# Message layers of a four-part graph network: fewer numbers read per group, SyncE waiting for the messages, and two matrix products per group that nobody reads

## The reference

```python
# layer 0
messages = relu(concat([x[source], x[target]]) @ W_msg + b_msg)
agg_sum = segment_sum(messages, target); counts = segment_sum(1, target)
# layer 1
messages = x[source] * norm[:, None]          # norm = deg_inv_sqrt of both ends
aggregated = segment_sum(messages, target)
```

## Time and profile before

| | us |
|---|---|
| median of 3 runs | 4893.81 (4892.45 to 4899.64) |
| the profiled execution | 4893.52 |
| its span, first to last instruction | 4891.7 |
| edge stage of layer 0, PE's first to last product | 672.9 to about 1222 |
| edge stage of layer 1, PE's first to last product | 1606.3 to about 1921 |

### The profile page before, as it was taken

The page is one execution under the profiler, slowest core; times in us unless marked ns, Lnnn a source line. Parts: engine busy times, 40 slices in busy tenths (PEclk is TensorE's granted clock), DMA queues, the critical chain, the costliest instruction groups (busy, mean ns, idle before and its releaser), DMA issues. The chain is left out here.

```text
span 4891.7 us, 53308 instructions
## 1 busy us (share of the span) xinstructions
PE 3136.8 (64%) x11864; PEld 1962.7 (40%) x11864; DVE 2778.7 (57%) x6341; ACT 968.3 (20%) x1858; POOL 2766.3 (57%) x2438
## 2 busy tenths in 40 slices
PE   4665745556796898766777577777636665655424
PEld 1223534445675787542222244555412222222213
DVE  7996742222455543666777458778755655444323
ACT  0332410000222220221222133333311221111100
POOL 0672057776111771327777588777327776787631
PEclk8876655555555555555555555555568887676665
DMA  6323621111554111551222423433212121333215
GB/s 257 74 70 126 251 83 24 24 24 20 144 151 134 26 26 41 196 188 38 41 41 42 62 44 85 100 78 77 75 47 37 36 37 33 31 30 29 24 15 108
DMA packets 337010, 363.26 MB, mean 74 GB/s; under 512 B 236961, under 2 KB 268843, under 8 KB 336864
## 3 DMA queue, kind: packets, MB, share of 16 engines
q1 hardware_dynamic: 219890, 261.92, 16.6%
q0 software_dynamic: 94096, 80.75, 13.5%
q10 hardware_dynamic: 22878, 18.95, 1.2%
HBM read 188.08 MB, written 188.36 MB: 77 GB/s over the span
## 5 line engine op out<-in xcount | busy, mean ns | idle before, releaser
L784 PE MATMUL e_ps<-e_msg,e_hot 128*128 x2408 | 571.2, 424 | 218.4 <-issue 212.6
L784 PEld LDWEIGHTS e_ps<-e_msg,e_hot 128*128 128x128 f32 x2408 | 530.1, 329 | 297.0 <-issue 297.0
L1674 POOL DMA_INDIRECT u_a<-attended,dst_end x392 | 487.2, 1243 | 146.7 <-issue 116.8
L2310 PE MATMUL d_pl<-d_hot,d_fields 128*65 128x512 f32 x712 | 481.5, 840 | 0.0
L757 DVE TENSOR_TENSOR sums<-e_ps,sums 128x455 f32 (+1 forms) x172 | 108.1, 629 | 552.8 <-PE e_ps L784 552.8
L700 POOL DMA_INDIRECT e_msg<-from_src,e_src x200 | 192.1, 961 | 290.2 <-DMA e_first<-lot_first 231.2
L2254 POOL DMA_INDIRECT flows<-d_out,d_end x160 | 263.9, 1649 | 106.4 <-issue 101.4
L1965 POOL DMA_INDIRECT list<-s_rec,s_place x200 | 199.4, 997 | 215.4 <-DVE s_place L1881 158.5
L2241 POOL DMA_INDIRECT d_near<-term,d_rec x196 | 191.5, 977 | 156.1 <-DMA d_rec<-list 96.7
L879 POOL DMA_INDIRECT a_ends<-h,a_src x200 | 216.2, 1081 | 103.2 <-issue 55.2
L1366 ACT ACTIVATE u_zt<-u_pt 128x256 f32<-128x256 f32 (+1 forms) x392 | 162.7, 431 | 560.8 <-PE u_pt L1266 560.6
(11 more groups left out here) (368 smaller groups left out, 7519.3 us busy)
## 6 DMA issues: line engine op xcount, KB each, us to landing
u_z<-h SPq DMA_DIRECT2D x28, 896.0 KB, 6.3
x<-sums SPq DMA_DIRECT2D x28, 896.0 KB, 7.9
u_x<-x SPq DMA_DIRECT2D x28, 896.0 KB, 7.5
terms<-s_zeros SPq DMA_DIRECT2D x16, 812.5 KB
s_key_row<-src_key SPq DMA_DIRECT2D x50, 256.0 KB
h1d<-u_h SPq DMA_DIRECT2D x14, 910.0 KB, 9.5
u_z<-h1d SPq DMA_DIRECT2D x14, 910.0 KB, 4.6
term<-u_h SPq DMA_DIRECT2D x14, 910.0 KB, 3.7
```

What stands on the lines that cost most here:

```text
L784: last = nc.tensor.matmul(to, hot[s][:, q, :], rows, start=False, stop=q == LOT - 1)
L1674: pool.indirect_dma_start(A[s][:, j, :], None, net.attended[:, :], bass.IndirectOffsetOnAxis(ap=net.dst_end[:, tile:tile + 1], axis=0)).th ...
L2310: last = nc.tensor.matmul(pl[0:WEIGHT + 1, :], fields[:, j, :], hot[:, j, :], start=j == 0, stop=j == J - 1)
```

## The change

The change has four parts, all in the edge stage and in the table that it reads.

1. The plan holds for each item the block number times 65 (`CV1`, the width of a row of `e_msg`), and PE reads only these seven numbers per group. The slot of item q is q minus the difference of its block number to that of the first item, so it is worked out in the register operations that every product has ahead of it anyway. For this the slots in PSUM are 65 columns wide in layer 1 too, and the clearing product writes 455 columns there, where it wrote 448.
2. The chunk number is read by SP, which waits for `msg_ready` and then counts the group in a new semaphore, `lot_ready`; PE waits for that.
3. In layer 1, PE issues 16 products ahead of the first group and two behind every group, each of bf16 ones and zeros (`identb`) with 512 columns, into a PSUM bank of their own (`unread`) that nobody reads.
4. DVE reads the 65-wide slots of a bank with their last column left out in layer 1.

```diff
+CV1 = C + 1
+def fill(nc, net, bank, count):
+
+    for _ in range(count):
+        nc.tensor.matmul(bank[:, :].rearrange("p (r c) -> p r c", c=P), net.identb[:, :],
+                         net.identb[:, :].unsqueeze(1).to_broadcast([P, J, P]), start=True, stop=True)
...
-                nc.vector.tensor_copy(lots[:, :, 0:LOT], block_in)
-                nc.vector.tensor_tensor(lots[:, :, LOT:2 * LOT], tile_in, tile_in[:, :, 0:1].to_broadcast([1, LOTS, LOT]), ALU.subtract)
+                nc.vector.tensor_scalar(lots[:, :, 0:LOT], block_in, float(CV1), None, ALU.mult)
+                nc.vector.tensor_copy(lots[:, :, LOT:2 * LOT], block_in)
...
-def lot_items(nc, pe, plan, g):
-
-    row = plan[0:1, g * PLAN:g * PLAN + 2 * LOT]
-    _, at = nc.values_load_multi_w_load_instructions(row, engines=(nc.tensor.engine,), min_val=0, max_val=BLOCKS - 1,
...
-    chunks = pe.value_load(plan[0:1, g * PLAN + CHUNK_AT:g * PLAN + CHUNK_AT + 1], min_val=1, max_val=CHUNKS)
-    return at[0:LOT], [u.with_bounds(min_val=0, max_val=LOT - 1) for u in at[LOT:2 * LOT]], chunks
+def lot_items(nc, plan, g):
+
+    row = plan[0:1, g * PLAN:g * PLAN + LOT]
+    _, rows = nc.values_load_multi_w_load_instructions(row, engines=(nc.tensor.engine,), min_val=0, max_val=CV1 * (BLOCKS - 1),
...
+    slots = [0] + [(CV1 * q + rows[0] - r).with_bounds(min_val=0, max_val=CV1 * (LOT - 1)) for q, r in enumerate(rows)][1:]
+    return rows, slots
...
+                sp.wait_ge(loaded, 16 * n_loads)
+                for g in range(LOTS):
+                    chunks = sp.value_load(plan[0:1, g * PLAN + CHUNK_AT:g * PLAN + CHUNK_AT + 1], min_val=1, max_val=CHUNKS)
+                    sp.wait_ge(msg_ready, chunks)
+                    sp.sem_inc(lot_ready, 1)
...
-                    nc.vector.tensor_tensor(here, ps[s][:, 0:LOT * wide].rearrange("p (u c) -> p u c", c=wide), here, ALU.add)
+                    nc.vector.tensor_tensor(here, ps[s][:, 0:LOT * CV1].rearrange("p (u c) -> p u c", c=CV1)[:, :, 0:wide], here, ALU.add)
...
-                blocks, slots, chunks = lot_items(nc, pe, plan, 0)
+                blocks, slots = lot_items(nc, plan, 0)
                 for g in range(LOTS):
...
-                    nc.tensor.matmul(ps[s][:, 0:LOT * wide], net.ones3[:, :], nothing[:, 0:LOT * wide], start=True, stop=False)
+                    nc.tensor.matmul(ps[s][:, 0:LOT * CV1], net.ones3[:, :], nothing[:, :], start=True, stop=False)
                     pe.wait_ge(hot_ready, g + 1)
-                    pe.wait_ge(msg_ready, chunks)
+                    pe.wait_ge(lot_ready, g + 1)
                     pe.sem_inc(pe_turn, 1)
...
+                    if g == 0 and not two:
+                        fill(nc, net, unread, 16)
...
                     last.then_inc(multiplied, 1)
+                    if not two:
+                        fill(nc, net, unread, 2)
```

More of the change, by code:

```diff
@@ L343, in _ @@
                     nc.vector.scalar_tensor_tensor(lane_of[:, part], tile_of[:, part], float(-P), spread_dst[:, n, 0:wide], ALU.mult, ALU.add)
-                block_in, tile_in = (row[0:1, 0:LOTS * LOT].rearrange("o (g q) -> o g q", q=LOT) for row in (block_of, tile_of))
-                nc.vector.tensor_copy(lots[:, :, 0:LOT], block_in)
-                nc.vector.tensor_tensor(lots[:, :, LOT:2 * LOT], tile_in, tile_in[:, :, 0:1].to_broadcast([1, LOTS, LOT]), ALU.subtract)
+                block_in = block_of[0:1, 0:LOTS * LOT].rearrange("o (g q) -> o g q", q=LOT)
+                nc.vector.tensor_scalar(lots[:, :, 0:LOT], block_in, float(CV1), None, ALU.mult)
+                nc.vector.tensor_copy(lots[:, :, LOT:2 * LOT], block_in)
                 nc.vector.tensor_copy(first_of[:, :], tile_of[0:1, 0:ITEMS:LOT])
                 v.drain()
-                nc.vector.tensor_scalar(lots[:, :, CHUNK_AT + 1], lots[:, :, LOT - 1], 2, None, ALU.logical_shift_right)
+                nc.vector.tensor_scalar(lots[:, :, CHUNK_AT + 1], lots[:, :, 2 * LOT - 1], 2, None, ALU.logical_shift_right)
                 v.drain()
@@ L672, in edge_sums @@
         ps = [ctx.enter_context(nc.psum_tensor(f"{n}ps{s}", [P, 512], F32)) for s in range(2)]
+        unread = ctx.enter_context(nc.psum_tensor(f"{n}unread", [P, 512], F32))
         if two:
@@ L774, in _ @@
                     pe.wait_ge(placed, g + 1)
-                    nc.tensor.matmul(ps[s][:, 0:LOT * wide], net.ones3[:, :], nothing[:, 0:LOT * wide], start=True, stop=False)
+                    nc.tensor.matmul(ps[s][:, 0:LOT * CV1], net.ones3[:, :], nothing[:, :], start=True, stop=False)
                     pe.wait_ge(hot_ready, g + 1)
-                    pe.wait_ge(msg_ready, chunks)
+                    pe.wait_ge(lot_ready, g + 1)
                     pe.sem_inc(pe_turn, 1)
-                    by_slot = ps[s][:, 0:LOT * wide].rearrange("p (u c) -> p u c", c=wide)
+                    if g == 0 and not two:
+                        fill(nc, net, unread, 16)
                     now = zip(blocks, slots)
+                    all_rows = msg[:, :, :].rearrange("p b c -> p (b c)")
                     for q, (b, u) in enumerate(now):
-                        rows = msg[:, bass.ds(b, 1), 0:wide].rearrange("p b c -> p (b c)")
-                        to = by_slot[:, bass.ds(u, 1), :].rearrange("p u c -> p (u c)")
+                        rows = all_rows[:, bass.ds(b, wide)]
+                        to = ps[s][:, bass.ds(u, wide)]
                         last = nc.tensor.matmul(to, hot[s][:, q, :], rows, start=False, stop=q == LOT - 1)
                         if q == LOT - 2 and g + 1 < LOTS:
-                            blocks, slots, chunks = lot_items(nc, pe, plan, g + 1)
+                            blocks, slots = lot_items(nc, plan, g + 1)
                     last.then_inc(multiplied, 1)
+                    if not two:
+                        fill(nc, net, unread, 2)
 def attention_sums(nc, net):
```

6 lines of the change are left out of this document (3 added, 3 removed).

## The result

| | us |
|---|---|
| before, median of 6 executions | 4892.95 (4884.41 to 4899.64) |
| changed, median of 6 executions | 4940.43 (4884.80 to 4944.69) |
| changed / before | 1.0062, 95% interval 1.0037 to 1.0086 |
| the changed kernel's profiled execution | 4884.80 (its span 4883.0) |

A forecast was written before the change was run, and what follows sets the result against it. It took PE at half clock, 3.66 us per group, to bound layer 1's edge stage. Full clock to 1705.2, waits 1.5 and 48 groups at 4.52 (217.0) end it at 1923.7, +2.3 us: 4896, range 4830 to 4908.

The forecast's parts named there:

- the sequencer: PE's sequencer, edge stage: shorter load saves 0.56 us, chunk number's load 0.305, its test 0.15; 1.0 us per group.
- the array's 2.44 us: Layer 1 group at full clock: products 1.65, clearing 0.30, two unread 0.44, change of width 0.05 us.
- stock: Layer 1: six chunks of messages, 9.8 groups, ready at 1612.4 when PE starts; used up by 1705.
- ceiling of 2.65 to 2.7: Layer 1: most that PE's sequencer needs per group after the change, in us; at most 3.66 before.
- falls at the first waits: Layer 1: clock drops when PE first waits for messages, near 1705, and does not return; 48 groups at 4.52 us follow.
- slower rival: Layer 1: clock does not hold even without gaps, all 86 groups cost 4.52 us; +80 us, 4973; chance 0.13.
- x: Layer 1: groups done at full clock until the stock of messages is used up; 38 at 2.44 us, 34 at 2.30.
- likeliest case: Layer 1: full clock until PE's first waits near 1705, half clock after; 4873 to 4904 us, chance 0.58.
- layer 1's limits: Layer 1 edge stage: PE at half clock, 3.66 us per group; close behind, ACT's messages, one chunk each 5.34 us.
- the sixteen: Layer 1: unread products ahead of the first group, 6.8 us at half clock; full clock expected when they are done.
- unchanged within 3 us: Layer 0's edge stage: paced by POOL, the shorter load giving back the hop of SP's wait; no change beyond 3 us.
- messages every 3.27 us: Layer 1: ACT's chunk each 5.34 us at 1.63 groups per chunk gives one group's messages each 3.27 us.

The follow-up runs named there:

- the kernel that stops at group 54: Changed kernel with fourteen numbers per group again, issuing the two unread products only for g < 54: median 4850.77 us, ratio 0.9901.
- the single stray execution: One execution of the changed kernel with three unread products per group instead of two: 6351 us, mean clock 1.0, left out of median and range.

## Why the prediction was wrong

**The step that failed: the sequencer.** The prediction said that the change saves 1.0 us of sequencer per group, with the register work left as it was ("six small operations too"), and put the array's 2.44 us above what was left. Three sizes in it were off. Seven numbers load in 1.057 us and fourteen in 1.337, so seven fewer save 0.28, not the 0.56 of a straight line through one number (0.305). The chunk number gives back 0.65, not 0.455. And the register work is not the same: 143 ns instead of 74 for each of six products, 0.41 us per group. On the 3.27 us of the run with unread products alone this makes 3.27 - 0.28 - 0.65 + 0.41 = 2.75, measured 2.79. The count of small operations was read as their price; what differs is that the new slot is a difference of two registers. With that arithmetic gone (fixed slots), every later number of the prediction came out: group, stock, fall, end. The prediction's ceiling of 2.65 to 2.7 could not show the mistake: it took 1.0 off 3.66, the array's half-clock time per group, and the sequencer's own 3.27 stood in no row of before.

**The second: the clock "falls at the first waits".** True where a group takes 2.43 or 2.69 us, or has three unread products or more. At 2.79 us with two it falls with no wait at all, after 28, 40 or 46 groups in the traces. The prediction had this as its slower rival, but let the first few groups decide it; the two are not separate cases. This is the step that took the time out of the range. By the prediction's own sum a group of 2.7 us ends the stage 21 us earlier, so a slow sequencer alone would have made the kernel faster; it became slower because at that pace the clock does not last until the first wait. What decides is PE's work in a given time, or the recurring gaps that go with less of it; a slower sequencer dilutes that work: 3.27 us per group lost the clock after four groups, 2.79 somewhere, 2.69 not before a wait in its profiled execution, in a range of 16 us for all six. The predicted 4896 was for one place of the fall; the changed kernel has no fixed one, and its medians, 4940 and 4923, lie 56 and 38 us above its best execution. That the best one, 4885, is within 11 us of 4896 is no success of the prediction: its fall came 39 us later, for another reason. Two slips in its sums changed nothing: with 2.30 us per group x is 33, not 34, and the end 1929, so the likeliest case's upper side is 4902, not 4904.

**Right:** layer 1's limits and stock; 4.52 at half clock; the sixteen raising the clock (1.00 in the window from 1616.7, though they took 4.8 us, 1611.89 to 1616.70, not 6.8, since it rose under them; 5.2 and 5.9 in the other two traces of this kernel); no return of the clock with two. **Wrong by its own bound:** layer 0 "unchanged within 3 us": its last group came at 1226.71 against 1218.86, of which 2 us were there at its start. Part of this may be chance, since the second trace of the kernel before has the last group at 1221.37, 5 us longer than its first from the start of ACT's first chunk. What SP's wait changes on all twelve traces is the gathers' durations; that it does so by shifting DVE's work against them is argued, and what the hop itself costs no trace prices. **Also off:** messages every 3.27 us. In this trace ACT's first, 29th and last chunk start at 1592.43, 1744.88 (the fall) and 1871.99:

```profile
1592.43 1.06 ACT L745 ACTIVATE e_msg<-e_msg 128x64 f32<-128x64 f32 x4 [20.49 <-DMA e_msg<-h1d,e_src]
...
1744.88 1.06 ACT L745 ACTIVATE e_msg<-e_msg 128x64 f32<-128x64 f32 x4 [4.49 <-DMA e_msg<-h1d,e_src]
...
1871.99 1.06 ACT L745 ACTIVATE e_msg<-e_msg 128x64 f32<-128x64 f32 x4 [5.83 <-DMA e_msg<-h1d,e_src]
```

That is 5.71 us per chunk, not 5.34: 5.44 ahead of the fall, 6.05 behind it. It cost the changed kernel nothing, as the clock had fallen before PE caught up. It ends the stage with four and five unread products; the kernel that stops at group 54 had 5.37 again.

The Trainium skill, "TensorE: Matmul & The Clock Gate", section "Why this matters for your kernels", names idle gaps longer than these as what brings the throttle back. The falls behind 0.23 us and behind 2.58 us (fixed slots) disagree with it.

**Open:** a trace of an execution at 4941 or above; what picks the place of the fall; whether PE's work per time or its recurring short gaps decide it; why the gathers' duration changes with PE's pace, up and down (that DVE's and POOL's work meet differently is argued from their durations, no run moved one against the other by itself); and the single stray execution.

## What to carry to other kernels

Price an address computation by the instruction's duration in the trace, not by its count of operations: trading loaded numbers for arithmetic on two registers lost here, seven numbers being worth 0.28 us and the arithmetic 0.41. Then ask what a quicker engine runs into: with the arithmetic gone as well, PE only met the end of its messages sooner, and the kernel was no faster than before. Work that is there to hold the clock needs a margin: measure it with one more and one fewer, and look at the spread of many executions, since one fast profile shows only one place of the fall. Where the clock can't be held, stop the unread work; its price doubles when the clock halves (0.22 us per product at full clock, 0.43 at half).

## What the runs showed of the hardware

- The clock fell from 1.00 to 0.50 with PE busy 121.1 of 127.7 us ahead of it and no gap over 0.24 us, at a different place in each of three traced executions of one program, each time behind the same one of a recurring six groups.
- With four or five unread products per group it came back to 1.00 at the end of a group's wide products or in the clearing product behind them (1804.25 with five, 1797.95 with four); with two it never did in these stages.
- Sequencer of PE: a load of 1, 7 and 14 numbers takes 0.305, 1.057 and 1.337 us; the register work ahead of a product 37 ns (block alone), 74 (block and slot, each a product with a constant) or 143 ns (slot as a difference of registers).
- The mean gather of layer 1 between 1615 and 1850 us took 1023 ns before, 1125 in the changed kernel, 1119 with the slots fixed, 1112 with four unread products, 1089 with fourteen numbers, 1199 with unread products alone at half clock, and 1215 with five unread products.
